# Loading the residual tiles ahead of phase E, and moving its hook behind the fourth Gt product

## The reference

```python
def _L0_attn_ref(x, w_lhs, w_rhs):
    scores = einsum('nsd,ntd->nst', x * w_lhs, x * w_rhs)
    return einsum('nst,ntd->nsd', softmax(scores, axis=2), x)

def _L0_ffn_ref(x, ...):            # xf = x as tokens by 1024
    shared = silu(xf @ shared_w1.T) * (xf @ shared_w2.T) @ shared_w3.T   # hidden 4096
    scores = sigmoid(xf @ router_w.T)                                    # 8 experts
    gates = scores * mask_of_top_2(scores + expert_bias)
    h1, h2 = split(einsum('td,ehd->teh', xf, w12))                       # hidden 1024 each
    routed = einsum('teh,edh->td', silu(h1) * h2 * gates, w3)            # all 8 experts, dense
    return shared + routed

x = x + layernorm(_L0_attn_ref(layernorm(x), w_lhs, w_rhs))
x = x + layernorm(_L0_ffn_ref(layernorm(x), ...))
```

## Time and profile before

| | |
|---|---|
| median of 3 runs | 2850.38 us |
| profiled execution | 2851.59 us, of which the slowest core's span is 2850.0 us |
| spans of the 8 cores | 2837.2 to 2850.0 us; core 5 is the profiled one |
| granted TensorE clock, mean | 0.962 to 0.967 |
| TensorE busy | 2460.6 us (86%) |
| VectorE busy | 1133.0 us (40%) |
| ScalarE busy | 440.2 us (15%) |
| moved by DMA | 204.8 MB, mean 72 GB/s |

### The profile page before, as it was taken

One profiled execution on the slowest core, in us unless ns is written; L12 is line 12 of the kernel. 1 busy time (PEld: TensorE's weight loads), 2 busy tenths in 40 slices (PEclk: granted clock), 3 DMA queues, 4 the chain that ended last, 5 costly groups with the idle time before them and its releaser, 6 DMA issues.

```text
span 2850.0 us, 48286 instructions; the slowest of 8 cores (2837.2 to 2850.0 us)
## 1 busy us (share of the span) xinstructions
PE 2460.6 (86%) x17186; PEld 1667.0 (58%) x17186; DVE 1133.0 (40%) x2455; ACT 440.2 (15%) x1048; POOL 243.0 (9%) x462
## 2 busy tenths in 40 slices
PE   0388887679999999999999969999999999999992
PEld 0123333256777766676776646677766677667661
DVE  3514236442322344444444443322244444444444
ACT  2022222201111111111111121111111111111111
POOL 0000001101001110011101110111011110111000
PEclk9999888889999999999999989999999999999996
DMA  5301017603355532555235544542355324552203
GB/s 151 104 1 38 30 56 145 128 6 49 51 82 90 90 51 46 84 90 86 40 54 90 90 81 119 97 65 50 65 90 90 62 43 75 90 90 45 45 1 118
DMA packets 80734, 204.80 MB, mean 72 GB/s; under 512 B 10537, under 2 KB 10858, under 8 KB 80490
## 3 DMA queue, kind: packets, MB, share of 16 engines
q0 software_dynamic: 65952, 151.11, 32.3%
q1 hardware_dynamic: 14546, 50.61, 5.5%
HBM read 335.91 MB, written 16.84 MB: 124 GB/s over the span
## 4 chain that ended last, share of the span: by engine, by line
PE 74%; DVE 16%; DMA 4%; issue 3%; DVEq 1%; ACT 1%; SPq 0%; POOL 0%; ACTq 0%; POOLq 0%
PE outp L756 21%; PE h1p L835 21%; PE h1p L845 20%; DVE acc L780 9%; PE stp L454 4%; DMA x2r<-x2s 2%; PE aop L483 2%; PE aop L486 2%; PE gatesp L820 1%; DMA xr<-x 1%; DVEq L1027 1%; PE stp L461 1%; DVE osb L962 1%; DVE acc L777 1%; DVE y1p L507 1%
## 5 line engine op out<-in xcount | busy, mean ns | idle before, releaser
L866 ACT ACTIVATE s1t<-h1p 128x256 f32<-128x256 f32 x768 | 295.5, 385 | 1885.7 <-PE h1p L845 1884.1
L876 DVE TENSOR_TENSOR t2t<-h1p,gb 128x256 f32<-128x256 f32 x512 | 217.5, 425 | 617.6 <-ACT s1t L866 560.7
L756 PE MATMUL outp<-sBw,Gt 128*128 128x512 bf16 x1536 | 409.2, 379 | 43.2 <-DVE acc L780 41.6
L756 PE MATMUL outp<-sAw,Gt 128*128 128x512 bf16 x1536 | 412.3, 381 | 33.5 <-DVE acc L780 29.4
L835 PE MATMUL h1p<-n2fm,sAw 128*128 128x256 bf16 x3072 | 402.6, 274 | 31.5 <-DVE Gt L883 31.5
L845 PE MATMUL h1p<-n2fm,sAw 128*128 128x256 bf16 x3072 | 401.6, 274 | 0.0
L845 PE MATMUL h1p<-n2fm,sBw 128*128 128x256 bf16 x3072 | 399.0, 273 | 0.0
L835 PE MATMUL h1p<-n2fm,sBw 128*128 128x256 bf16 x3072 | 398.7, 273 | 0.0
L835 PEld LDWEIGHTS h1p<-n2fm,sAw 128*128 128x128 bf16 x3072 | 297.9, 98 | 142.5 <-issue 45.1
L835 PEld LDWEIGHTS h1p<-n2fm,sBw 128*128 128x128 bf16 x3072 | 297.7, 98 | 111.4 <-issue 10.6
L845 PEld LDWEIGHTS h1p<-n2fm,sAw 128*128 128x128 bf16 x3072 | 302.3, 98 | 36.4
(11 more groups left out here) (103 smaller groups left out, 1064.9 us busy)
## 6 DMA issues: line engine op xcount, KB each, us to landing
sAw<-w12t POOLq DMA_DIRECT2D x64, 512.0 KB, 16.8
sBw<-w12t POOLq DMA_DIRECT2D x64, 512.0 KB, 15.4
xr<-x SPq DMA_DIRECT2D x48, 512.0 KB, 4.4
sAw<-w3t POOLq DMA_DIRECT2D x64, 256.0 KB, 28.6
sBw<-w3t POOLq DMA_DIRECT2D x64, 256.0 KB, 28.1
x2s<-x2t SPq DMA_DIRECT2D x16, 512.0 KB, 5.2
sAw<-w1t POOLq DMA_DIRECT2D x32, 256.0 KB, 13.3
sAw<-w2t POOLq DMA_DIRECT2D x32, 256.0 KB, 14.1
```

Source lines behind the costliest of these rows:

```text
L756: inst = e.matmul(outp[tt][:, half * 512:(half + 1) * 512], Gt[jj_ % 4][:, tt * P:(tt + 1) * P], w3t_[j_][:, half * 512:(half + 1) * 512], ...
L866: E("scalar", lambda e, jj=jj, v=evv: e.activation(s1t[jj % 3][:], h1p[jj % 3][:, 0:TBLK], ACT.Silu).then_inc(S["s_ev"], 1))
L876: E("vector", lambda e, jj=jj, tb=tb: e.tensor_mul(t2t[jj % 2][:], h1p[jj % 3][:, TBLK:2 * TBLK], gate_b[tb % 2][:]), drain=True)
```

## The change

Three things change. First, the load of x2r is taken out of `emit_phase_e_tile` into a function `issue_x2r`, which does nothing for a tile already issued; tile gi + 2 is issued right behind the store of tile gi, and its waits for `s_sp0`, `s_sp1`, `s_acc` and `s_out` are gone (what is left is SP's own wait for the add of tile gi, `s_ot`, ahead of its store, which is the last reader of that x2r buffer). Second, tiles 0 and 1 are issued by a new hook at the head of the last chunk of the first pass, with a wait for `s_gh` because of the shared address. Third, the hook with the two phase E tiles is called at j = 4 of each token block of chunk 12, where it was called before j = 0.

```diff
-    def emit_pass(pss, mid_hook=None):
+    def emit_pass(pss, mid_hook=None, lastck_hook=None):
...
+            if lastck_hook is not None and ck == NCHUNK_P - 1:
+                lastck_hook()
             for tb in range(NTB):
-                if mid_hook is not None and ck == 0:
-                    mid_hook(tb)
...
+                    if mid_hook is not None and ck == 0 and j == 4:
+                        mid_hook(tb)
                     if jj >= 3:
                         W("tensor", S["s_ev2"], jj - 2)
...
+    x2r_issued = set()
+
+    def issue_x2r(gi):
+        if gi in x2r_issued or gi >= NPASS * NACC:
+            return
+        x2r_issued.add(gi)
+        if gi < 2:
+            W("sync", S["s_gh"], 16)
+            W("sync", S["s_sp0"], sp_all[0])
+            W("sync", S["s_sp1"], sp_all[1])
+        dma("sync", x2r[gi % 2][:], x2s_tiled[gi, :, :], s_x2rP[gi % 2])
+
     def emit_phase_e_tile(pss, ii, rdy):
         if True:
             gi = pss * NACC + ii
-            W("sync", S["s_sp0"], sp_all[0])
-            W("sync", S["s_sp1"], sp_all[1])
-            W("sync", S["s_acc"], acc_done_pass[pss])
-            if gi >= 2:
-                W("sync", s_outP[gi % 2], 16 * (gi // 2))
-            dma("sync", x2r[gi % 2][:], x2s_tiled[gi, :, :], s_x2rP[gi % 2])
...
             W("sync", S["s_ot"], otv)
             dma("sync", out_tiled[gi, :, :], out_sb[gi % 2][:], s_outP[gi % 2])
+            issue_x2r(gi + 2)
...
-            emit_pass(pss)
+            emit_pass(pss, lastck_hook=lambda: (issue_x2r(0), issue_x2r(1)))
```

More of the change, by code:

```diff
@@ L946, in emit_phase_e_tile @@
             gi = pss * NACC + ii
-            W("sync", S["s_sp0"], sp_all[0])
-            W("sync", S["s_sp1"], sp_all[1])
-            W("sync", S["s_acc"], acc_done_pass[pss])
-            if gi >= 2:
-                W("sync", s_outP[gi % 2], 16 * (gi // 2))
-            dma("sync", x2r[gi % 2][:], x2s_tiled[gi, :, :], s_x2rP[gi % 2])
+            assert gi in x2r_issued, f"x2r tile {gi} not prefetched"
             si = gi
```

## The result

The changed kernel takes 2800.46 us (median of 8 runs, 2796.81 to 2802.43) where the kernel before took 2850.4 (median of 6, 2848.01 to 2854.89); the ratio is 0.9823, 95% interval 0.9811 to 0.9835, some 50 us. The forecast was 2803 with 2797 to 2812.

What follows compares the result with a forecast made beforehand. TensorE bounds the kernel (74% of the chain), with avoidable losses at chunk 12's start and the tail. Core 2: 2848.7 - 26.8 - 19.4 = 2802.5, plus 1.6, less 1.2, forecast 2803 us, range 2797 to 2812.

Steps and rivals of the forecast that it cites:

- Place one: Start of the second pass (chunk 12), last row sum to fourth copies: 37.8 us over a stall-free run, 29.2 gained on core 5.
- first wait of 5.2 us: Start of pass 2: TensorE's wait for Gt 0 falls from 24.55 to 5.2 us, with ScalarE's table load ahead.
- one slow restart: Start of pass 2: after TensorE's first wait, blocks run slowly at the lower clock; 2.9 us charged.
- The 0.5 charged for hook 1: Chunk 12, token block 1: tile 3's x2r load may come late, a wait of 0 to 5 us; 0.5 taken.
- the spare: Chunk 12's later hooks at j = 4: VectorE finishes Gt 4 1.6 us before TensorE needs it.
- (a): Last chunks of pass 0: x2r of tiles 0 and 1 loaded early, beside weights; cost 0, at most 12 us.
- The tail: Phase E after the last matmul: two tiles in flight, the end falls from 2850.0 to 2830.6, 19.4 us gained.
- Steps of 3.2: Tail, five tiles after tile 10: 3.2 us each with stores, where a tile took 5.87.
- tile 10: Tail: its load is issued at 2806.36 as tile 9's was, so its add runs 2810.3 to 2811.6.
- the tail chokes: Rival, tail: eight cores load and store at once, load latency rises from 3.84 to 6.1, step 4.0; 2809 us, chance 14%.
- The estimate of 5.6: Tail, by the skill's rule on memory at high load: load latency 5.6, step 3.8, time 2808 us.
- The slower rival: Chunk 12 runs throughout at the low clock after stalls at every hook; 84 us more, 2887 us, chance 2%.

Runs made afterwards that it cites:

- the two halves of the change: Against the kernel before: only the hook moved to j = 4, ratio 0.9975; only the x2r loads changed, one execution, 2808.35 us.
- the dose: Changed kernel with 1, 2 and 4 extra VectorE normalizations (0.97 us each) in hooks 1, 2 and 3; one execution, 2807.31 us.
- the late statistics: Changed kernel with phase E statistics and ScalarE's table loads at j = 4 of pass 2's first token block, its tiles at j = 6; ratio 0.9808.
- the fastest version: Changed kernel plus the late statistics, tail x2r preloaded, tail normalization on ScalarE, last-chunk row sums behind Gt 2 and Gt 3; ratio 0.9728.

## Why the prediction was right

*Place one.* Expected were a first wait of 5.2 us (5.3), one slow restart, no wait at the other hooks, and 124.94 - 29.2 = 95.7 (95.2). The 0.5 charged for hook 1 did not occur, and the restart cost 2.4 where 2.9 was charged. The terms are shown one by one: the loads by the two halves of the change, the spare by the dose, what is left by the late statistics.

*The early loads, (a).* They were costed at 0, and with or without them place one is 94.2 to 95.2; that they also gain nothing was not said. The prediction read x2r as late because of when it was issued; the sharper reading is that load g + 1 stood behind store g.

*The tail.* This is the term that was mis-sized: 19.4 expected, 46.5 - 29.4 = 17.1 measured, 18.1 in the mean of the cores. Steps of 3.2 were nearly right on the profiled core (3.26) and 0.2 short in the mean of all (3.4). What failed there was tile 10: I let its add start as soon after the load's issue as tile 9's did before, 2806.36 to 2810.28. (That is 3.92 us; the 3.84 of the prediction is a slip.) It began 5.95 after (2774.27 to 2780.22), and 4.5 to 6.9 after on the eight cores, 5.3 in the mean, where tile 9's load had taken 4.1 in the mean. Two loads and two stores are then in flight, which I take for the cause, but it is shown for half of it at most: in the version with the tail's loads one store later, tile 10's load has only one store beside it and still takes 4.7 in the mean. (Its normalization waited 1.61 for a store meanwhile, beside that load and not on the path.)

That is the rival "the tail chokes" in a third of its size: a load lands in 5.3, not 6.1. After tile 11 the loads land faster: by the starts of their adds, 4.4 to 5.6 us after issue, 5.0 in the mean, and with 1.7 from one add's start to the next load's issue (1.7 + 5.0) / 2 = 3.3 is the step that was measured. The DMA share was 0.72 over the tail, where I had said over 90%. The Trainium skill (DMA: Bandwidth & Descriptors, Latency and other measured facts) says that memory answers more slowly at high load. The estimate of 5.6 that I worked out by it is near the 5.3 that was measured; the step of 3.8 and the time of 2808 are not, and no run here separates the memory's share of the landing.

*Which core is slowest.* The prediction carried core 5's and core 2's starts at place one over (last row sum at 1681.1 and 1681.3). In the profile after, the slowest core, 4, has 1678.75, the latest of the eight. In the runs in which nothing is changed ahead of it the cores' last row sums lie between 1667.7 and 1682.5, and the latest of each run between 1675.8 and 1682.5. That is 2.3 us in favour and cancels the tail's 2.3. So part of the agreement of 2803 with 2800.5 is luck: the terms were right to 0.5 and 2.3, and the start of the slowest core scatters by more than that.

*A term that was not there.* From the fourth copies to the tail it was 997.5 us on all eight cores before, and it is 995.8 on five of them now (see the last section), 1.1 us less in the mean. The prediction took this stretch as fixed. The profiled core has 997.3, so its span was not helped by it.

*The slower rival.* A wait of 5.3 us brought one slow restart of a few blocks and nothing lasting. That chunk 12 runs at 1.2 GHz throughout was never near.

## What to carry to other kernels

Two buffers give nothing while the load for the second is queued behind the store of the first: look at what is in flight at once, in the issuing engine's order, before adding prefetch. An engine that works in order should do what another waits for first, and side work where the waiting engine has buffers left; how much fits is blocks queued times duration, and here it could be worked out to half a microsecond. When the transfers overlap, start the sum of a chain with the landing time of crowded transfers (5.3 us here), not with that of the order before (3.9).

## What had not been expected of the hardware

The clock can fall after far shorter waits than the 3.7 us of the prediction, and it does not always. In the last chunk of a pass TensorE waits 1.7 and 0.4 us for outp, and on core 4 of the changed kernel, once:

```profile
2699.27 0.38 PE L756 MATMUL outp<-sBw,Gt 128*128 128x512 bf16 x1 [1.68 <-DVE acc L780]
2700.05 0.58 PE L756 MATMUL outp<-sBw,Gt 128*128 128x512 bf16 x1 [0.40 <-DVE acc L780]
2700.43 1.91 PE L837 MATMUL h1p<-n2fm,sBw 128*128 128x256 bf16 x8
```

The granted clock of 2698 to 2702 us is 0.73, and the blocks here take 1.6 us longer than on core 0, where the same two waits (1.68 and 0.40) are followed by blocks of 1.04. From the fourth copies to the tail it is 997.3 us on core 4 and two others and 995.8 on the remaining five, a difference of this size. In the kernel before, all eight cores have slow blocks at this place, once each, and 997.5 us; with only the loads changed it is 997.4 or 997.5 on seven. In the fastest version, where the wait of 1.68 is one of 0.3, all eight have 991.9 to 992.0, so no core has lost anything there.

Longer waits behave no more evenly. Behind 3.04 us (core 7 with only the hook moved) the blocks take 1.03, behind 2.15 on one core of the dose 1.92. The waits of 3.7 us and more that I looked at, at place one in the kernel before, the changed kernel and the version with only the hook moved, all brought slow blocks. What decides it in between stays open; it wasn't tried by itself.
